# A graph-convolution kernel on one Trainium2 core: TensorE sums the last bucket ahead of the next bucket's counts, transposes and lookups

## The chip, the cores and the metric

The kernel runs on one core of one Trainium2 chip. A core has five engines with a queue of instructions each: TensorE (PE; its weight loads are listed apart as PEld), VectorE (DVE), ScalarE (ACT), GpSimd (POOL) and SyncE (SP). They run side by side and order themselves by semaphores. SBUF is the on-chip memory, PSUM (eight banks here, `bank[0]` to `bank[7]`) takes the results of matmuls, and DRAM is reached by DMAs. SP and POOL issue nearly all DMAs of this kernel. The metric is the device time of one launch in microseconds (us), lower is better.

## The reference, cut to what matters

There are 6250 nodes with 128 features, 200000 edges (src, dst, type), and 16 edge types.

```python
h = jnp.maximum(_layernorm(x, axis=-1), 0.0)
# inside the layer: src = edge source, rel = edge type, dst = edge target, embeddings = h
semb = embeddings[src] @ tokeys.T
oemb = embeddings[src] @ toqueries.T
pemb = relations[rel]
dots = jnp.sum(semb * pemb * oemb, axis=1) / e
values = jnp.exp(dots)
fr = src + n * rel
rowsum = jax.ops.segment_sum(values, fr, num_segments=r * n)
values = values / rowsum[fr]
msgs = values[:, None] * embeddings[dst]
output = jax.ops.segment_sum(msgs, fr, num_segments=r * n).reshape(r, n, e)
weights = jnp.einsum('rb,bij->rij', comps, bases_w)
out = jnp.einsum('rij,rnj->ni', weights, output)
x = x + jax.nn.relu(out)
```

Two edges with the same (src, type) have the same value, so the weight of an edge follows from how many edges of its type its source node has.

## The kernel before, in words

**Stage one** (up to about 420 us of the trace) sorts the edges by source into 49 buckets of 128 nodes (`NB = 49`), writes them to DRAM as records, and writes `Z`, the 16 transformed messages of each node, to DRAM.

**Stage two**, which the change touches, goes over the 49 buckets. A bucket has room for 36 tiles (`G = 36`) of 128 edges. In the order of one bucket b:

- SP (function `bucket`, lines 326 to 357) stores the rows of bucket b-2 when they are finished, joins two pieces of the record stream by a DRAM to DRAM DMA, waits for it, and loads the records of bucket b (`RL`).
- PE `turn_records` transposes them into PSUM (line 1277), DVE `records` and `gather_index` (lines 746, 784) make integers of them, the row numbers of Z among them.
- POOL `gather` (line 501) fetches one row of Z per edge, one indirect DMA for a tile. Tile 0 is shared with the bucket before and is not fetched. The page counts 1568 of these DMAs, 32 for a bucket. They fill one of two buffers, `Gbuf[par]`. A gather starts when PE has summed the bucket two before (`acc`), since that one used the same buffer.
- PE `tables` counts edges per node and type with one-hot matmuls (line 1286, 9 of them) and transposes the one-hot of types (line 1296, 18). DVE `own_counts` (792 to 798) takes its part of the counts. PE `sum_counts` (1307, 1308) finishes them.
- DVE `weights` (807 to 823) makes the weights. ACT `bucket` (line 1111) copies the transposes out of PSUM, spreads the one-hot of the next bucket (1088), and copies the shared tile between the gather buffers (`shared_tile`, 1101).
- PE `lookups` (line 1317, 18 matmuls in five groups) looks up each edge's weight, DVE `weighted_onehot` (line 833, 9 operations) puts it into the one-hot `OW`, and the two go in step: PE's group k waits for DVE's work on group k-2.
- PE `aggregate` (line 1329) sums weight times message over the 36 tiles into `bank[2]`. A float32 matmul shows as two passes, so this is 72 PE rows. DVE `finish` (line 841) adds x and applies the relu.

The loops are software pipelined. All orders are written by hand, one list for each engine, and each engine goes through its list in order. PE's list for one step b (`stepb`, lines 1343 to 1353) is: turn the records of b+1, tables of b, sum_counts of b, aggregate of b-1, lookups of b. DVE's list for a step b is: records and gather_index of b+1, own_counts of b, weights of b, tables of b+1 (one-hots, 753 to 776), finish of b-1, weighted_onehot of b. The change leaves DVE's list and SP's list as they are.

A gather's landing is told by semaphores. The tiles 1 to 29 (`PACED = 30`) raise one of four landing semaphores `land[q]`, by groups of eight tiles, and the tiles above raise `gat[par]`. POOL waits before each group of eight for the landing of the group two before it (lines 491 to 500). PE waits for each group before it sums it, and ACT waits for all before it copies the shared tile.

Of the kernel before, what the change touches and what calls it, by code (L numbers as in the profile page):

```python
# [32 lines left out]
def program(nc, x, src, dst, rel, tokeys, toqueries, relations, comps, bases_w, out):  # L33
# [16 lines left out]
    G = 36  # L50
# [23 lines left out]
    with ExitStack() as ctx:  # L74
# [308 lines left out]
        def _(pool):  # L383
# [96 lines left out]
            with pool.If(bad < 1):  # L480
                def gather(b, par, turn):
                    n = pool.value_load(ROWI[0:1, bass.ds(b, 1)], min_val=FLOOR, max_val=G)
# [7 lines left out]
                    def group_landed(b, q):  # L490
                        pool.wait_ge(land[q], (b + 1) * 16 * len(group_tiles[q]))
                        pool.sem_inc(s["pool_go"], 1)

                    def tile(k):
                        if k < PACED and k == group_tiles[k // GROUP][0]:

                            if k >= 2 * GROUP:
                                group_landed(b, k // GROUP - 2)
                            elif dyn(b) or b >= 1:
                                group_landed(b - 1, k // GROUP + 2)  # L500
                        g.indirect_dma_start(Gbuf[par][:, k, :], None, Z, bass.IndirectOffsetOnAxis(IDX[turn][:, k:k + 1], 0))\  # L501
                            .then_inc(land[k // GROUP] if k < PACED else gat[par], 16)
# [29 lines left out]
        def _(dve):  # L532
# [188 lines left out]
            chain(v.tensor_scalar(col(6), col(1), float(PACED), None, ALU.subtract), "nt")  # L721
# [235 lines left out]
        def _(act):  # L957
# [124 lines left out]
            with act.If(bad < 1):  # L1082
# [7 lines left out]
                def shared_tile(b, par):  # L1090
# [3 lines left out]
                    for q in range(4):  # L1094
                        act.wait_ge(land[q], (b + 1) * 16 * len(group_tiles[q]))
# [35 lines left out]
        def _(pe):  # L1131
# [121 lines left out]
            pe.wait_ge(s["nt"], 33)  # L1253
# [14 lines left out]
            with pe.If(bad < 1):  # L1268
# [53 lines left out]
                def aggregate(b, par):  # L1322
# [8 lines left out]
                    for q in range(4):  # L1331
                        pe.wait_ge(land[q], (b + 1) * 16 * len(group_tiles[q]))
                        for k in group_tiles[q]:
                            add(k, start=(k == FIRSTK))
# [4 lines left out]
                    add(0)  # L1339
                    for k in range(PACED, G):  # L1340
                        mm = add(k, stop=(k == G - 1))
                    mm.then_inc(s["acc"], 1)

                def stepb(b, par, rl_total):
                    if dyn(b) or b + 1 < NB:
                        turn_records(b + 1, 1 - par, rl_total)
                    if dyn(b) or b < NB:
                        tables(b, par)
                        sum_counts(b)
                    if dyn(b) or b >= 1:  # L1350
                        aggregate(b - 1, 1 - par)
                    if dyn(b) or b < NB:
                        lookups(b)
# [58 lines left out]
```

## Time and profile before

| | |
|---|---|
| median of 3 runs | 3075.16 us (3070.01 to 3075.73) |
| the profiled execution's own time | 3092.01 us |
| its span in the profile | 3090.2 us |
| mean granted TensorE clock | 0.674 of full speed |
| PE busy | 1511.4 us (49%) |
| PE weight loads busy | 1113.9 us (36%) |
| DVE busy | 1354.5 us (44%) |
| ACT busy | 462.4 us (15%) |
| POOL busy | 1652.3 us (53%) |
| mean DMA traffic | 55 GB/s, 170.48 MB |

The page gives each engine's busy time and its share of the span. No engine is busy for much over half of the span, so the time lies in waits. In a row of the page's fifth part, the two numbers behind the first bar are the busy time and the mean length of one instruction, and what stands behind the second bar is the idle time just before these instructions with what ended most of it. In a timeline each row has the start, the length, the engine, the line, and in square brackets the idle time before it and what ended it. "remote" says that the semaphore's update came at a time that fits no instruction's end, and "issue" that the profile shows nothing that was waited for. The end of a matmul is modelled, not recorded.

### The profile page before, as it was taken

The numbers are of one execution on the slowest core, as the hardware profiler recorded it, in microseconds if no ns is written. First come the engines' busy times: TensorE is split into PE (matmuls) and PEld (weight loads), VectorE is DVE, ScalarE is ACT, GpSimd is POOL, SyncE is SP. The second block draws the span as 40 slices with busy tenths as digits, with TensorE's granted clock in tenths as the row PEclk, the third lists the DMA queues.
The fourth block names the chain that finished last, engine by engine and source line by source line (L and its number), as shares of the span: only waits on it lengthen the run. The fifth ranks groups of instructions, "written<-read, shape, count | busy, mean of one in ns | idle before, by whom it ended". The sixth has DMA issues, their size and how long they took to land.

```text
span 3090.2 us, 33040 instructions
## 1 busy us (share of the span) xinstructions
PE 1511.4 (49%) x9072; PEld 1113.9 (36%) x9122; DVE 1354.5 (44%) x2384; ACT 462.4 (15%) x918; POOL 1652.3 (53%) x1804
## 2 busy tenths in 40 slices
PE   4999922444344444345444443444444444434345
PEld 3666612332233323233332332333332333323234
DVE  7999934334243433334243342434334343433333
ACT  4666601000010101000010100101000010100000
POOL 3444454655556464655646465564655556464653
PEclk8999965666666666656666666656656666666667
DMA  5444411111111111111111111111111111111111
GB/s 153 157 156 156 156 48 32 45 38 44 42 38 45 36 46 36 46 38 41 45 35 45 37 44 42 39 44 36 46 38 43 43 38 46 36 45 36 45 42 29
DMA packets 99826, 170.48 MB, mean 55 GB/s; under 512 B 32491, under 2 KB 48612, under 8 KB 99575
## 3 DMA queue, kind: packets, MB, share of 16 engines
q0 software_dynamic: 51776, 104.48, 13.1%
q1 hardware_dynamic: 47672, 65.57, 6.3%
q10 hardware_dynamic: 352, 0.14, 0.0%
q8 instruction: 10, 0.16, 0.0%
q14 instruction: 16, 0.13, 0.0%
HBM read 112.24 MB, written 59.59 MB: 56 GB/s over the span
## 4 chain that ended last, share of the span: by engine, by line
another core or an unknown queue 37%; issue 23%; DVE 19%; PE 15%; SPq 2%; DMA 1%; DVEq 1%; ACT 0%; POOLq 0%; ACTq 0%
PE bank L1209 6%; DVE arena L833 4%; DVE CX L798 3%; PE bank L1194 2%; DVE stage L776 2%; PE bank L1286 2%; DVE WC L809 1%; PE bank L1329 1%; DVE pay_all L792 1%; PE bank L1162 1%; DVE OHR L774 1%; PE bank L1317 1%; DVE pay_all L823 1%; DMA RL<-bucket_streams 1%
## 5 line engine op out<-in xcount | busy, mean ns | idle before, releaser
L501 POOL DMA_INDIRECT arena<-Z_messages,IDX x1568 | 1483.2, 946 | 1162.3 <-issue 967.3
L1329 PE MATMUL bank<-arena 128*128 128x128 f32 x3528 | 682.1, 350 | 696.4 <-issue 687.2
L1329 PEld LDWEIGHTS bank<-arena 128*128 128x128 f32 x3528 | 620.1, 260 | 759.3 <-issue 757.6
L807 DVE TENSOR_SCALAR WC<-bank 128x128 f32<-128x128 f32 x49 | 14.3, 292 | 1106.9 <-remote 1080.6
L1111 ACT COPY pay_all<-bank 128x1024 bf16<-128x1024 bf16 x147 | 108.0, 807 | 2152.5 <-remote 2131.8
L1317 PE MATMUL bank<-pay_all 128*128 128x256 bf16 x882 | 178.7, 346 | 309.0 <-DVE arena L833 236.6
L833 DVE TENSOR_TENSOR arena<-stage,bank 128x512 f32<-128x512 bf16 x441 | 268.8, 681 | 7.5 <-remote 7.1
L776 DVE TENSOR_TENSOR stage<-bank,NLF 128x4608 bf16<-128x4608 f32 x49 | 242.4, 4948 | 0.0
L1317 PEld LDWEIGHTS bank<-pay_all 128*128 128x128 bf16 x882 | 86.2, 113 | 383.6 <-DVE arena L833 292.1
L1286 PE MATMUL bank<-stage,OHR 128*128 128x512 bf16 (+1 forms) x392 | 176.3, 613 | 21.1 <-issue 16.7
L1209 PE MATMUL bank<-WT,HT 128*128 128x512 f32 x392 | 185.5, 613 | 0.0
L1277 PE MATMUL bank<-identf,RL 36*128 36x36 f32 x49 | 14.3, 291 | 338.9 <-DMA RL<-bucket_streams 228.2
L453 POOL DMA_INDIRECT bucket_streams<-REC,IDXW x50 | 54.2, 1084 | 199.4 <-ACT REC L1030 188.5
L792 DVE TENSOR_TENSOR pay_all<-bank,T 128x512 f32<-128x512 f32 x98 | 63.1, 686 | 203.7 <-issue 120.0
L1088 ACT COPY ORD<-OHR 128x2304 bf16<-128x2304 bf16 x49 | 103.5, 2112 | 268.8 <-DVE OHR L774 268.8
L746 DVE CAST RI<-bank 128x36 int32<-128x36 f32 x49 | 9.6, 196 | 299.3 <-PE bank L1277 166.6
L1277 PEld LDWEIGHTS bank<-identf,RL 36*128 36x128 f32 x49 | 8.8, 179 | 360.3 <-issue 360.3
L1042 ACT COPY stage<-bank 128x512 f32<-128x512 f32 x196 | 114.9, 586 | 35.7 <-PE bank L1209 34.6
L1307 PE MATMUL bank<-identf,VR 128*128 128x128 f32 x98 | 32.1, 423 | 160.0 <-DVE CX L798 95.6
L1286 PEld LDWEIGHTS bank<-stage,OHR 128*128 128x128 bf16 (+1 forms) x441 | 56.6, 138 | 127.9 <-issue 122.4
L1209 PEld LDWEIGHTS bank<-WT,HT 128*128 128x128 f32 x392 | 64.4, 189 | 82.5 <-ACT stage L1042 59.1
L798 DVE TENSOR_REDUCE CX<-pay_all 128x128 f32<-128x1024 f32 x49 | 91.4, 1865 | 0.0
(210 smaller groups left out, 1710.9 us busy)
## 6 DMA issues: line engine op xcount, KB each, us to landing
Z_messages<-stage SPq DMA_DIRECT2D x192, 256.0 KB
arena<-Z_messages,IDX POOLq DMA_INDIRECT x1568
X<-in_x SPq DMA_DIRECT2D x4, 768.0 KB, 12.9
out<-O SPq DMA_DIRECT2D x48, 64.0 KB
bucket_streams<-bucket_streams SPq DMA_DIRECT2D x97, 18.0 KB
arena<-in_L_gnn_bases_w SPq DMA_DIRECT2D x1, 1024.0 KB, 15.0
bucket_streams<-arena SPq DMA_DIRECT2D x1, 882.0 KB
RL<-bucket_streams SPq DMA_DIRECT2D x49, 18.0 KB
```

The costliest lines, as they stand in the source:

```text
L501: g.indirect_dma_start(Gbuf[par][:, k, :], None, Z, bass.IndirectOffsetOnAxis(IDX[turn][:, k:k + 1], 0))\
L776: v.tensor_tensor(OHN[par], over_b(iotaP, G), over_t(NLF[:], P), ALU.is_equal)\
L792: v.tensor_tensor(own8[:, 4 * h:4 * h + 4, :], bank[h][:, :].rearrange("p (t n) -> p t n", t=4), over_t(T8[:, 4 * h:4 * h + 4], P), ALU.mu ...
L798: v.tensor_reduce(CX[:], own8.rearrange("p t n -> p n t"), AX.X, ALU.add).then_inc(s["cx"], 1)
L833: v.tensor_tensor(OW[:, n:n + 4, :], OHN[par][:, n:n + 4, :], bank[LKB[k % 2][h]][:, :].rearrange("p (t n) -> p t n", t=4), ALU.mult)\
L1042: a.copy(ZS[par][:, k * 512:(k + 1) * 512], bank[4 + k % 2][:, :]).then_inc(s["z_sb"], 1)
L1088: a.copy(ORD[:], OHR[par][:].unsqueeze(2).broadcast_to([P, G, 4, R])).then_inc(s["ord"], 1)
L1111: a.copy(ORT[:, 8 * k:8 * k + n, :].rearrange("p k e -> p (k e)"), bank[TPB[k]][:, :].bitcast(BF16)[:, 0:n * P]).then_inc(s["oht"], 1)
L1209: t_.matmul(bank[4 + k % 2][:, :], HT[par][:], WT[:, 4 * k:4 * k + 4, :].rearrange("p r i -> p (r i)"), start=True, stop=True).then_inc(s[ ...
L1286: mm = t_.matmul(bank[k % 2][0:n * R, :], OHR[par][:, k // 2 * 8:k // 2 * 8 + n, :].rearrange("p k r -> p (k r)"), OHN[par][:, 4 * k:4 * k ...
L1317: mm = t_.matmul(bank[LKB[k % 2][m // 2]][:, m % 2 * 2 * P:(m % 2 + 1) * 2 * P], ORT[:, 4 * k + m, :], BD[:].rearrange("p t n -> p (t n)") ...
L1329: return t_.matmul(bank[2][:, 0:EMB], OW[:, k, :], Gbuf[par][:, k, :], start=start, stop=stop)
```

## The change

Four edits belong together.

- PE's list for a step is now: turn the records of b+1, aggregate b-1, tables of b, sum_counts of b, lookups of b. The aggregate comes first, ahead of the tables.
- In all buckets but the last, every tile raises `gat[par]`, the totals of `gat` in the number table are made for that (one more small DVE operation in the set-up, and the last bucket's total is less by the 29 paced tiles, counted with tile 0 as 30), and the landing groups remain only in the last bucket.
- PE waits once for the whole gather of the bucket, then for the shared tile, and sums the 36 tiles in one go, tile 0 first. Only in the last bucket does it still go group by group. ACT waits for `gat` alone.
- POOL no longer waits for the landing of earlier groups while it issues a gather.

```diff
             with pool.If(bad < 1):
                 def gather(b, par, turn):
+                    last = not dyn(b) and b == NB - 1
                     n = pool.value_load(ROWI[0:1, bass.ds(b, 1)], min_val=FLOOR, max_val=G)
                     pool.wait_ge(s["idx"], b + 1)
...
                     pool.sem_inc(s["pool_go"], 1)
 
-                    def group_landed(b, q):
-                        pool.wait_ge(land[q], (b + 1) * 16 * len(group_tiles[q]))
-                        pool.sem_inc(s["pool_go"], 1)
-
                     def tile(k):
-                        if k < PACED and k == group_tiles[k // GROUP][0]:
-
-                            if k >= 2 * GROUP:
-                                group_landed(b, k // GROUP - 2)
-                            elif dyn(b) or b >= 1:
-                                group_landed(b - 1, k // GROUP + 2)
                         g.indirect_dma_start(Gbuf[par][:, k, :], None, Z, bass.IndirectOffsetOnAxis(IDX[turn][:, k:k + 1], 0))\
-                            .then_inc(land[k // GROUP] if k < PACED else gat[par], 16)
+                            .then_inc(land[k // GROUP] if last and k < PACED else gat[par], 16)
...
-            chain(v.tensor_scalar(col(6), col(1), float(PACED), None, ALU.subtract), "nt")
+            chain(v.tensor_scalar(col(6), PARI[:, 0:1], float(NB - 1), float(1 - PACED), ALU.is_equal, ALU.mult), "nt")
+            chain(v.scalar_tensor_tensor(out=col(6), in0=col(1), scalar=-1.0, in1=col(6), op0=ALU.add, op1=ALU.add), "nt")
...
                     g_total = act.value_load(ROWI[0:1, bass.ds(b + (1 + par) * NB, 1)], min_val=16 * (FLOOR - PACED), max_val=16 * G * (NB + 1) // 2)
-                    for q in range(4):
-                        act.wait_ge(land[q], (b + 1) * 16 * len(group_tiles[q]))
                     act.wait_ge(gat[par], g_total)
...
-            pe.wait_ge(s["nt"], 33)
+            pe.wait_ge(s["nt"], 34)
...
-                    for q in range(4):
-                        pe.wait_ge(land[q], (b + 1) * 16 * len(group_tiles[q]))
-                        for k in group_tiles[q]:
-                            add(k, start=(k == FIRSTK))
+                    if not dyn(b) and b == NB - 1:
+                        for q in range(4):
+                            pe.wait_ge(land[q], 16 * len(group_tiles[q]))
+                            for k in group_tiles[q]:
+                                add(k, start=(k == FIRSTK))
+                        rest = range(PACED, G)
+                    else:
+                        rest = range(FIRSTK, G)
                     pe.wait_ge(gat[par], g_total)
                     pe.sem_inc(s["pe_go"], 1)
                     if dyn(b) or b >= 1:
                         pe.wait_ge(s["shared"], b)
-                    add(0)
-                    for k in range(PACED, G):
+                    add(0, start=(rest[0] == FIRSTK))
+                    for k in rest:
                         mm = add(k, stop=(k == G - 1))
                     mm.then_inc(s["acc"], 1)
 
                 def stepb(b, par, rl_total):
                     if dyn(b) or b + 1 < NB:
                         turn_records(b + 1, 1 - par, rl_total)
+                    if dyn(b) or b >= 1:
+                        aggregate(b - 1, 1 - par)
                     if dyn(b) or b < NB:
                         tables(b, par)
                         sum_counts(b)
-                    if dyn(b) or b >= 1:
-                        aggregate(b - 1, 1 - par)
-                    if dyn(b) or b < NB:
                         lookups(b)
```

What stands on TensorE in the loop over buckets, before. `identf,RL` is turn_records, `stage,OHR` and `identb,ORD` are tables, `CX,RS` is sum_counts, `arena` is aggregate, `pay_all` is lookups.

```order
L1277 MATMUL bank<-identf,RL 128x36 [waits s_w]
L1286 MATMUL bank<-stage,OHR 128x512 [waits s_ow]
L1296 MATMUL bank<-identb,ORD 128x128 [waits s_ord,s_oht]
L1308 MATMUL bank<-CX,RS 128x128
L1329 MATMUL bank<-arena 128x128 [waits s_land0]
L1329 MATMUL bank<-arena 128x128 [waits s_land1]
L1329 MATMUL bank<-arena 128x128 [waits s_land2]
L1329 MATMUL bank<-arena 128x128 [waits s_land3]
L1329 MATMUL bank<-arena 128x128 [waits s_gat1,s_shared]
L1317 MATMUL bank<-pay_all 128x256 [waits s_bd]
```

The same place of TensorE's list in the changed kernel (its lines are 10 lower):

```order
L1267 MATMUL bank<-identf,RL 128x36 [waits s_w]
L1319 MATMUL bank<-arena 128x128 [waits s_gat1,s_ow,s_o,s_shared]
L1319 MATMUL bank<-arena 128x128 x35
L1276 MATMUL bank<-stage,OHR 128x512 [waits s_ow]
L1286 MATMUL bank<-identb,ORD 128x128 [waits s_ord,s_oht]
L1298 MATMUL bank<-CX,RS 128x128
L1307 MATMUL bank<-pay_all 128x256 [waits s_bd]
```

The 36 tiles of the sum moved from behind the counts to ahead of them, right behind the turn of the next records, and four waits inside the sum went.

What GpSimd issues for one bucket in the loop, before:

```order
L501 DMA arena<-Z_messages,IDX 128x128 [waits s_land2]
L501 DMA arena<-Z_messages,IDX 128x128 x6
L501 DMA arena<-Z_messages,IDX 128x128 [waits s_land3]
L501 DMA arena<-Z_messages,IDX 128x128 x7
L501 DMA arena<-Z_messages,IDX 128x128 [waits s_land0]
L501 DMA arena<-Z_messages,IDX 128x128 [waits s_land1]
```

And in the changed kernel, for the same bucket:

```order
L492 DMA arena<-Z_messages,IDX 128x128 [waits s_acc,s_shared]
L492 DMA arena<-Z_messages,IDX 128x128 x29
L496 COMPARE_AND_BRANCH
L492 DMA arena<-Z_messages,IDX 128x128
```

The waits for landings went, and nothing else of it moved.

## Rows read from the trace of the kernel before

**Rows 1.** The page's costliest groups: DVE's first weight operation, ACT's copies of transposes.

```profile
L807 DVE TENSOR_SCALAR WC<-bank 128x128 f32<-128x128 f32 x49 | 14.3, 292 | 1106.9 <-remote 1080.6
L1111 ACT COPY pay_all<-bank 128x1024 bf16<-128x1024 bf16 x147 | 108.0, 807 | 2152.5 <-remote 2131.8
```

**Rows 2.** Timeline of PE, one bucket: start, length, line, count, idle before.

```profile
1516.36 0.29 PE L1277 MATMUL bank<-identf,RL 36*128 36x36 f32 x1 [4.56 <-DMA RL<-bucket_streams]
1517.01 3.76 PE L1286 MATMUL bank<-stage,OHR 128*128 128x512 bf16 x8 [0.36 <-issue]
1520.70 1.56 PE L1296 MATMUL bank<-identb,ORD 128*128 128x128 bf16 x18
...
1524.90 0.58 PE L1308 MATMUL bank<-CX,RS 128*128 128x128 f32 x2
1525.71 2.96 PE L1329 MATMUL bank<-arena 128*128 128x128 f32 x13 [0.23 <-issue]
...
1535.58 0.37 PE L1329 MATMUL bank<-arena 128*128 128x128 f32 x1 [2.43 <-issue]
...
1549.59 6.88 PE L1329 MATMUL bank<-arena 128*128 128x128 f32 x49 [0.33 <-issue]
```

**Rows 3.** Timeline of DVE, the same bucket.

```profile
1507.24 0.28 DVE L841 SCALAR_TENSOR_TENSOR O<-bank,X 128x128 f32<-128x128 f32 x1
...
1522.38 1.86 DVE L798 TENSOR_REDUCE CX<-pay_all 128x128 f32<-128x1024 f32 x1
1549.70 0.29 DVE L807 TENSOR_SCALAR WC<-bank 128x128 f32<-128x128 f32 x1 [25.45 <-remote]
...
1553.65 0.73 DVE L823 SCALAR_TENSOR_TENSOR pay_all<-W,X,WC 64x128 bf16<-64x128 bf16 x2
...
1561.43 0.28 DVE L841 SCALAR_TENSOR_TENSOR O<-bank,X 128x128 f32<-128x128 f32 x1
1561.63 5.48 DVE L833 TENSOR_TENSOR arena<-stage,bank 128x512 f32<-128x512 bf16 x9
```

**Rows 4.** Timeline of ACT, the same bucket.

```profile
1549.72 2.20 ACT L1111 COPY pay_all<-bank 128x1024 bf16<-128x1024 bf16 x3 [44.91 <-remote]
```

**Rows 5.** Timeline of POOL: one gather's first and last tile, the next one's first.

```profile
1504.61 0.95 POOL L501 DMA_INDIRECT arena<-Z_messages,IDX  x1 [14.63 <-issue]
...
1543.38 0.95 POOL L501 DMA_INDIRECT arena<-Z_messages,IDX  x1 [0.30 <-issue]
1557.37 0.95 POOL L501 DMA_INDIRECT arena<-Z_messages,IDX  x1 [13.05 <-issue]
```

**Rows 6.** Chain of waits, 1400 to 1620 us: SP's table reads (start, length).

```profile
1508.43 0.28 SPq L321
...
1512.03 0.70 SPq L326
```

**Rows 7.** Timeline of SP, next bucket: store of finished rows, load of records.

```profile
1561.91 0.39 SPq L357 DMA_DIRECT2D out<-O  x1
...
1583.69 0.71 SPq L327 DMA_DIRECT2D RL<-bucket_streams  x1
```

**Rows 8.** Timeline of PE, next bucket, whose records came late.

```profile
1582.02 0.29 PE L1277 MATMUL bank<-identf,RL 36*128 36x36 f32 x1 [16.03 <-DMA RL<-bucket_streams]
...
1604.34 9.23 PE L1329 MATMUL bank<-arena 128*128 128x128 f32 x56 [1.02 <-issue]
```

**Rows 9.** Timeline of PE: first bucket's sum, end of the last but one's, last's.

```profile
525.83 9.36 PE L1329 MATMUL bank<-arena 128*128 128x128 f32 x72
...
3062.69 7.04 PE L1329 MATMUL bank<-arena 128*128 128x128 f32 x40 [1.72 <-issue]
...
3075.80 10.97 PE L1329 MATMUL bank<-arena 128*128 128x128 f32 x72 [1.40 <-DVE arena L833]
```

**Rows 10.** Stretches: length, PE, PEld, DVE, ACT, POOL busy (instructions), clock, DMA share, GB/s.

```profile
560.00:565.00 5.00, 0.64 (x2) 0.31 (x2) 0.00 (x0) 0.00 (x0) 3.78 (x5) 0.74 0.20 52
...
580.00:585.00 5.00, 4.63 (x18) 3.91 (x18) 2.95 (x9) 2.20 (x3) 0.00 (x0) 0.50 0.00 0
```

## The prediction, made before the changed kernel ran

> **What bounds the kernel now.** I read the page first, for who waits. DVE's first weight operation was idle 1106.9 us ahead of its 49 instructions, and ACT's copies of the transposes 2152.5 us, and both waits are put down to "remote" [rows 1]. What DVE waits for there is sum_counts, and ACT the transposes, both of them PE's. So I read one bucket engine by engine. PE ended the transposes at 1522.26 (1520.70 plus 1.56) and sum_counts at 1525.48 [rows 2]. DVE went on at 1549.70 [rows 3] and ACT at 1549.72 [rows 4], within 0.02 us of each other and 24 to 27 us after PE had finished. In between PE itself nearly stood still: 13 passes of the sum went in 2.96 us, then ten passes with up to 2.4 us of idle before each, and from 1549.59 the last 49 in 6.88 us [rows 2]. Three engines are let go in the same 0.15 us. That is no wait of the program, it is PE's completions coming through late.
>
> Next I asked what else has these borders. POOL's gather runs from 1504.61 to 1544.33 [rows 5]. The flow returns 45.0 us after the gather's first DMA and 5.3 us after its last. SP shows the other border: a read of the number table takes 0.28 us at 1508.43 and 0.70 us at 1512.03 [rows 6], 7.4 us into the gather. Between the two stores and loads of SP, from 1561.91 to 1583.69, the same few steps [rows 7] that are quick early in a gather take 20 us. While a gather runs the DMA engines are busy only 0.20 of the time, and once it is over they are idle while PE bursts [rows 10], so transfer bandwidth isn't it. I call the time from 7 us into a gather until 45 us into it the thin stretch: PE's and SP's steps pass at 0.7 us each [rows 6] to 1.4 (a load and a matmul in the 0.37 plus 2.43 us [rows 2]), after a first few dozen rows of PE's that still pass. DVE shows none of it: 5.48 us for nine operations [rows 3] holds in both.
>
> The period follows. From the end of one sum, 1503.7 (0.9 before rows 5's first DMA), to the end of the next, 1556.47, it is 0.9 to start the gather, 45.0 to the end of its thin stretch, 6.9 for the remaining passes. Over 47 periods, from 535.19 to 3069.73 [rows 9], the mean is 53.9 us. The gather's own 40 us, the sum of all engines' work and the landing waits end nothing.
>
> **What the change takes away, adds and moves.** I count from the end of a sum (0), the next gather starts at 0.9 and flow returns at 46.0.
>
> *The landing waits on POOL, ACT and PE.* POOL's DMAs stand 1.25 us apart (1543.38 less 1504.61, over 31), waits or not, and the sum of b-1 reads a gather that ended a whole period earlier. Price 0. Bounds: if unpaced gathers emptied the thin stretch altogether the bound would be rival 2, if they widened it, the 7.4 us before it begins could go, which costs where sum_counts is caught in it (rival 3). One small DVE operation in the set-up is 0.3 us at most by DVE's rows.
>
> *The sum ahead of the tables.* This turns the order of a period round. Before, weights were ready long before they were asked for, and between two sums stood lookups, DVE's one-hots, the next records, the tables. Now between sum b-1 and sum b stand, in this order: tables of b, 3.76 plus 1.6 us [rows 2]; DVE's own counts, 1520.77 to 1524.24, 3.5 us [rows 2, 3], overlapping the transposes; sum_counts, 1.3 us, out at 8.5. That is about where the thin stretch begins (8.3 from the end of the sum), and PE's first few dozen rows in it pass, so ACT and DVE should get these two signals in time. That is the change's gain: the waits of rows 1 all but go. Then DVE: weights 4.7 us (1549.70 to 1554.38), its one-hots for the next bucket 7.0 us (to 1561.43), only then finish of b-1, at 20.5, and from 20.8 the weighted one-hots with PE's lookups, 5.5 us at best [rows 3], so 26.3.
>
> But these last ones fall into the thin stretch. Three lookup groups of 4, 4 and 2 matmuls with their loads, some 25 rows with PE's register steps, stand behind waits for DVE, and DVE waits for each of them. At 0.7 us they cost 10 to 17 us: 36 to 43.
>
> *SP, which the diff doesn't touch, is moved most.* It loads the records of b+2 behind the store of b-1, which waits for DVE's finish of b-1. Before, finish came 3.5 us after the sum (1507.24 against 1503.7), 2.7 into the gather, and the records' turn at 1516.36, 9.1 later. Now finish comes at 20.8, well inside the thin stretch. Started 4.5 us into the gather, the same steps brought the records to PE at 1582.02 [rows 8], 20.1 after the store [rows 7]. SP issues some 25 instructions there, two DMAs and their landings among them. Started at 21, all of them are thin: from 17.5 us (25 by 0.7) over 20 (rows 7 and 8's own, which began before the stretch did) to 35 (25 by 1.4), less what the flow's return at 46.0 spares. The records arrive between 38 and 48, and I take 46.5: the row's 20 had a quick start, and PE's lookups now want the same stretch. Price of this step in the old order was 0, hidden under the sum; in the new order PE turns b+2's records directly ahead of sum b, so whoever is last gives the sum's start: 47.0.
>
> *The sum itself* then runs whole. 72 passes took 9.36 and 10.97 us outside gathers [rows 9], and bursts after an idle stretch 0.14 to 0.165 us a pass (49 in 6.88, 56 in 9.23) [rows 2, 8], 10.1 to 11.9 for 72. The granted clock of the stretch after such a wait is 0.50 [rows 10], the 1.2 GHz level, so I take 11.5. Before, 23 of the 72 had gone through before the flow came back, and that head start is what is lost.
>
> Period: 47.0 + 11.5 = 58.5 against 53.9.
>
> *Ends.* The first sum can start at 517.6, behind the first lookups, instead of 525.8, and ends 6.6 us earlier, 528.6. In the last period no records are turned, the lookups' 36 to 43 gives the start, so it is some 53. After the sum of bucket 47 the last bucket's whole chain now follows: before, 20.5 us (3090.2 less 3069.73), now 13 more for tables, counts and weights, 33.5.
>
> Sum: 528.6 + 46 x 58.5 + 53 + 33.5 = 3306 of span, plus 1.8 around it, 3308 by the profile's own time. The profiled execution (3092.0) was 0.55% above the median 3075.16, so the median comes to 3290.
>
> On PE's run-ahead the Trainium skill, "TensorE: Matmul & The Clock Gate", section "Architectural detail: the array is 16× 32×32, not 1× 128×128", gives TensorE's queue as 64 instructions deep. That agrees with the trace as I read it: behind the held transposes stood 8 rows of sum_counts and about 46 of the sum. By that rule 32 passes with their loads would fit, were the queue empty when sum b starts inside the thin stretch, 9 more than rows 2's 23, and rival 1's sum would gain 1.3 us a period on them.
>
> The same skill, "Trainium Kernel Development and Optimization", section "Key Constraints", says that DMAs of SP, ACT and POOL run on the same 16 engines and interleave. It speaks against dropping the pacing: SP's small loads would stand among more gathers. At the share of 0.20 [rows 10] it adds nothing I can price, and the sum leaves it out.
>
> **The rivals.**
>
> 1. *The sum gets its head start, slightly faster.* Place: SP's loads in the thin stretch. If they pass at 0.7 us a step or less, the records are there by 38, the lookups as well, and PE puts 30 passes through or into its queue before 46.0. Then 42 remain, 7.0 us, and the period is 53.0: 528.6 + 47 x 53.0 + 33.5 = 3053, a median of 3038. It decides at a start of the sum before about 41; at 44 the period is 56 and the time 3175. For it: rows 7 and 8's stretch took 20 us, part of it thin. Against it: that stretch began at 4.5, where the first steps pass quickly.
> 2. *The thin stretch goes with the pacing.* Then POOL's 32 x 1.25 + 0.9 = 41 us is the period: 528.6 + 47 x 41 + 33.5 = 2489, 2477 by the median. Against it: nothing in the rows ties the 7.4 us or the 45.0 us to a landing wait.
> 3. *sum_counts is caught in the thin stretch.* It needs to come out by about 8.5 and the stretch opens at 8.3 or a little before. If it is held to 46.0, weights, one-hots and weighted one-hots (17.2 us) and the sum follow: 75 a period, 4045. Held by half, with its 22 rows at 0.7 us, DVE ends 15 us later, SP's finish too, and the sum starts at 53: 64.5, 3565. For it: the transposes and sum_counts are more rows than the few dozen. Against it: rows 2's counts, issued 12.4 us into a gather, were still picked up at once, since DVE's own counts were done 3.5 us behind them [rows 3].
>
> **Chances.** Forecast with its middle (3140 to 3400): 0.62. Rival 1 (below 3140): 0.20, two thirds of it faster. Rival 2: 0.04. Rival 3: 0.14. The range for 8 in 10 is 3050 to 3520, and the forecast's own is 3140 to 3400. A difference under 0.2% can't be told from none in this kernel. Faster by more than that 0.17, within it 0.03, slower by more 0.80.
>
> **What would show it.** In the profile after: ACT's copies of transposes start within a few us of the transposes (the 2131.8 of "remote" gone), DVE's first weight operation likewise, 3 to 4 us behind the counts. DVE's finish stands 20 us behind the sum's last pass, not 3.5. PE's turn of the records waits for the records' DMA and stands 44 to 48 us behind the sum, with the sum in one row of x72, 10 to 12 us long. POOL's gaps between gathers grow from 13 to 18 us. SP's steps from the store to the load take 20 us or more. The forecast is wrong if the turn of the records isn't late, if the sum shows 20 to 30 passes ahead of the flow's return, or if SP's steps inside a gather take 0.3 us.

## The result, and the profile after

The changed kernel took 3284.4 us (median of 4, 3281.8 to 3287.03), the kernel before 3075.09 (median of 4) beside it: a ratio of 1.069, 95% interval 1.0677 to 1.0702. Forecast were 3290 us and slower. The profiled execution has a span of 3283.8 us, where the steps of the prediction gave 3306, and a mean granted clock of 0.657.

The sum over the periods, by the trace after: first sum done at 528.0 (forecast 528.6), 46 periods of 58.17 (58.5), a last one of 48.8 (53), and 31.2 behind it (33.5). Before, the mean period was 54.0.

The page's costliest groups after, to be held against [rows 1] (its lines are 8 to 10 lower):

```profile
L492 POOL DMA_INDIRECT arena<-Z_messages,IDX x1568 | 1485.4, 947 | 1343.6 <-PE bank L1319 858.0
L1319 PE MATMUL bank<-arena 128*128 128x128 f32 x3528 | 515.7, 319 | 62.5 <-issue 44.1
L1267 PE MATMUL bank<-identf,RL 36*128 36x36 f32 x49 | 14.2, 290 | 1094.3 <-DMA RL<-bucket_streams 1094.3
L1101 ACT COPY pay_all<-bank 128x1024 bf16<-128x1024 bf16 x147 | 108.0, 807 | 2225.2 <-PE bank L1286 2174.0
```

DVE's first weight operation no longer appears among the large waits: of its 1106.9 us of idle all but some 50 have gone (45.8 us over 42 buckets, shown with E10). In their place PE itself waits 1094.3 us ahead of 49 turns of records, for the records' DMA. ACT still idles as long as before, but now because the transposes come late in the period, not because their signal does. A total of idle time doesn't tell these two apart, the timeline does.

One bucket after, PE, DVE, ACT and SP (start, length, line, count, idle before), beside [rows 2 to 4, 7]:

```profile
1505.11 10.29 PE L1319 MATMUL bank<-arena 128*128 128x128 f32 x72 [0.87 <-issue]
1515.23 2.22 PE L1276 MATMUL bank<-stage,OHR 128*128 128x512 bf16 x9
1517.39 1.18 PE L1286 MATMUL bank<-identb,ORD 128*128 128x128 bf16 x18
...
1519.05 2.20 ACT L1101 COPY pay_all<-bank 128x1024 bf16<-128x1024 bf16 x3 [45.47 <-PE bank L1286]
...
1521.69 0.39 PE L1298 MATMUL bank<-CX,RS 128*128 128x128 f32 x2
1522.11 0.29 DVE L799 TENSOR_SCALAR WC<-bank 128x128 f32<-128x128 f32 x1 [1.07 <-PE bank L1298]
...
1534.00 0.28 DVE L833 SCALAR_TENSOR_TENSOR O<-bank,X 128x128 f32<-128x128 f32 x1
1534.19 3.69 DVE L825 TENSOR_TENSOR arena<-stage,bank 128x512 f32<-128x512 bf16 x6
1534.48 0.40 SPq L357 DMA_DIRECT2D out<-O  x1
...
1545.06 1.29 DVE L825 TENSOR_TENSOR arena<-stage,bank 128x512 f32<-128x512 bf16 x2 [7.18 <-remote]
1550.66 0.69 DVE L825 TENSOR_TENSOR arena<-stage,bank 128x512 f32<-128x512 bf16 x1 [4.31 <-remote]
1552.88 0.70 SPq L322 DMA_DIRECT2D bucket_streams<-bucket_streams  x1
1561.32 0.38 SPq L327 DMA_DIRECT2D RL<-bucket_streams  x1
1563.18 0.29 PE L1267 MATMUL bank<-identf,RL 36*128 36x36 f32 x1 [24.63 <-DMA RL<-bucket_streams]
```

From the sum's last pass at 1515.40: the weights begin at +6.7 with their signal prompt, finish at +18.6, the weighted one-hots are done at +36.0, the turn comes at +47.8 and the next sum starts at 1564.31. POOL's gaps between gathers:

```profile
1516.20 0.95 POOL L492 DMA_INDIRECT arena<-Z_messages,IDX  x1 [18.03 <-PE bank L1319]
...
1574.83 0.95 POOL L492 DMA_INDIRECT arena<-Z_messages,IDX  x1 [18.91 <-PE bank L1319]
```

And the chain of waits there (start, length, what), inside the gather that began at 1516.20: each step of SP's, idle or not, is 0.70 us or twice that, where early in a gather the same table read took 0.28 [rows 6]:

```profile
1539.41 0.70 SPq L333
1540.11 0.70 issue
...
1560.58 0.70 SPq L326
1561.32 1.62 DMA RL<-bucket_streams
1562.98 0.04 issue
1563.03 0.05 SPq L321
```

The last step of 0.70 us ends at 1561.28, 45.1 us behind the gather's first DMA, and from the next step after the records' landing, at 1562.98, they are 0.04 us. The stretches of that bucket (length, PE, PEld, DVE, ACT, POOL busy, clock, DMA share, GB/s): while the stretch lasts, PE is busy for 4.56 of 38 us at the 1.2 GHz level, and the DMA engines at 0.19.

```profile
1523.00:1561.00 38.00, 4.56 (x18) 2.01 (x18) 15.86 (x28) 2.31 (x2) 25.00 (x27) 0.50 0.19 50
1564.00:1574.00 10.00, 9.69 (x73) 9.68 (x74) 0.08 (x1) 0.00 (x0) 0.00 (x0) 0.83 0.01 2
```

### The profile page after: what moved, and what is told of

The parts are those of the page before. It is cut to its first block, busy times and chain, and to the rows that moved or that the text cites. A ratio compares the mean times of both kernels' runs of the same rounds, so it can differ in the third digit from the quotient of the medians.

```text
span 3283.8 us, 32426 instructions
## 1 busy us (share of the span) xinstructions
PE 1307.7 (40%) x9121; PEld 984.4 (30%) x9122; DVE 1367.4 (42%) x2385; ACT 462.9 (14%) x918; POOL 1654.5 (50%) x1804
## 4 chain that ended last, share of the span: by engine, by line
issue 57%; SPq 22%; PE 14%; DVE 4%; DMA 2%; another core or an unknown queue 1%; DVEq 0%; ACT 0%; POOLq 0%; ACTq 0%
SPq L322 6%; PE bank L1199 5%; SPq L321 5%; SPq L326 3%; PE bank L1319 3%; PE bank L1184 2%; SPq L362 2%; SPq L333 1%; DMA RL<-bucket_streams 1%; PE bank L1152 1%; SPq L327 1%; DVE stage L768 1%; SPq L337 1%; SPq L341 1%
## 5 line engine op out<-in xcount | busy, mean ns | idle before, releaser
L1319 PE MATMUL bank<-arena 128*128 128x128 f32 x3528 | 515.7, 319 | 62.5 <-issue 44.1
L1319 PEld LDWEIGHTS bank<-arena 128*128 128x128 f32 x3528 | 506.9, 234 | 69.6 <-issue 67.9
L825 DVE TENSOR_TENSOR arena<-stage,bank 128x512 f32<-128x512 bf16 x441 | 277.3, 683 | 526.2 <-remote 416.5
L1307 PE MATMUL bank<-pay_all 128*128 128x256 bf16 x882 | 223.6, 414 | 632.8 <-DVE arena L825 321.5
L1267 PE MATMUL bank<-identf,RL 36*128 36x36 f32 x49 | 14.2, 290 | 1094.3 <-DMA RL<-bucket_streams 1094.3
L1307 PEld LDWEIGHTS bank<-pay_all 128*128 128x128 bf16 x882 | 99.2, 132 | 743.6 <-DVE arena L825 370.9
L1276 PE MATMUL bank<-stage,OHR 128*128 128x512 bf16 (+1 forms) x441 | 110.9, 387 | 0.0
L1184 PE MATMUL bank<-pay_all,stage 125*80 125x100 f16 x1600 | 81.5, 208 | 2.3 <-DVE stage L655 2.3
L1184 PEld LDWEIGHTS bank<-pay_all,stage 125*80 125x80 f16 x1600 | 78.8, 117 | 2.4 <-DVE stage L655 2.4
L1297 PE MATMUL bank<-identf,VR 128*128 128x128 f32 x98 | 24.3, 333 | 133.3 <-DVE CX L790 103.4
```

The costliest lines, as they stand in the source:

```text
L825: v.tensor_tensor(OW[:, n:n + 4, :], OHN[par][:, n:n + 4, :], bank[LKB[k % 2][h]][:, :].rearrange("p (t n) -> p t n", t=4), ALU.mult)\
L1184: mm = t_.matmul(DM[:, h * NS:(h + 1) * NS], OHS[par][:, t, :], PAY[par][:, t, :, :].rearrange("p x b -> p (x b)"), start=(t % HC == 0), s ...
L1276: mm = t_.matmul(bank[k % 2][0:n * R, :], OHR[par][:, k // 2 * 8:k // 2 * 8 + n, :].rearrange("p k r -> p (k r)"), OHN[par][:, 4 * k:4 * k ...
L1307: mm = t_.matmul(bank[LKB[k % 2][m // 2]][:, m % 2 * 2 * P:(m % 2 + 1) * 2 * P], ORT[:, 4 * k + m, :], BD[:].rearrange("p t n -> p (t n)") ...
L1319: return t_.matmul(bank[2][:, 0:EMB], OW[:, k, :], Gbuf[par][:, k, :], start=start, stop=stop)
```

## The experiments

They ran in five sessions, and the sessions fall into two kinds. In the second and third the kernel before took 3085.6 and 3072.0 us. In the first, fourth and fifth it took 2393.0, 2392.9 and 2396.9, the same program, each time with spreads of 6 us or less. I call them the thin and the free sessions; the first result (3075.09) is of the thin kind. The second (thin) and the fifth (free) list the same chip number, so what decides between them isn't known.

### Thin sessions

**E7, the changed kernel again.** No edit.

> The changed kernel itself, in one session with the kernel before. The first four experiments ran where the kernel before took 2393 us and not 3075, and where PE's and SP's steps weren't slowed while a gather ran; GpSimd's 32 DMAs of 1.25 us a bucket were then the bound. Theory A (the loss is nothing but SP's record load caught in the thin stretch): where the kernel before takes about 2393, finish of b-1 stands 20.5 us behind the sum, the records' turn 9.1 us later, the sum takes 0.9 and 10, together 40.5 us, just GpSimd's own 40.2 to 41, so 2390 to 2430, a ratio of 1.00 to 1.015. Where the kernel before takes about 3075, 3284 again. Rival B (the new order costs by itself, through a longer chain of PE and DVE work): the 4 us a bucket stay in any session, so 2393 + 49 x 4 = 2590.

Measured: 3300.15 us against 3085.6, ratio 1.0699 (1.0681 to 1.0717). The first result again; the question of the free session stayed open, since this one was thin.

**E11, PE's order alone.** The kernel before, with

```diff
+                    if dyn(b) or b >= 1:
+                        aggregate(b - 1, 1 - par)
                     if dyn(b) or b < NB:
                         tables(b, par)
                         sum_counts(b)
-                    if dyn(b) or b >= 1:
-                        aggregate(b - 1, 1 - par)
```

> The kernel before with only PE's order changed (sum of b-1 ahead of tables of b); landing groups and all waits stay. Theory A (the order is the whole loss): where the kernel before takes 3075 to 3086, 1.065 to 1.075 of it, 3280 to 3310. Theory C (the whole sums and the lost pacing carry part of it, a quarter or more): 1.02 to 1.05. If the kernel before takes 2393, 2393 again.

Measured: 3286.77 against 3072.03, ratio 1.0697 (1.0679 to 1.0715). Theory A: the order is all of it. Its page has the wait of the changed kernel:

```profile
L1277 PE MATMUL bank<-identf,RL 36*128 36x36 f32 x49 | 14.2, 290 | 1098.8 <-DMA RL<-bucket_streams 1088.1
```

Landing groups, POOL's pacing and whole sums move nothing that can be measured, as their price of 0 said. (The reverse, old order with whole sums, ran only in a free session, E2.)

**E10, finish first.** The changed kernel, with SP's store and load let go early:

```diff
+                    if dyn(b) or 1 <= b:
+                        finish(b - 1, 1 - par)
                     own_counts(b)
...
-                    if dyn(b) or 1 <= b:
-                        finish(b - 1, 1 - par)
```

> The changed kernel with DVE's finish of b-1 put ahead of its own counts of b, on a chip where (if it is as in the last session) the kernel before takes 3075 to 3086 and the changed one 1.070 of it. Theory A (the loss comes from SP's record load, that starts 21 us behind the sum because it waits for finish): finish comes about 1 us behind the sum, SP's steps start early in the gather and end before 20 us, the turn of the records no longer sets the start of the sum; the lookups with DVE's weighted one-hots do (36 by the trace of the changed kernel, a little later for the 0.3 us of finish), or flow's return where they are held. Sum to sum 36 to 46 plus 0.9 plus 10, so 47 to 56: 528 + 47 x 51.5 + 31 = 2980, range 2790 to 3150, clearly under the changed kernel's 3300. Theory B (the sum's place inside the stretch is what costs, whoever starts it): no change, 3270 to 3310. If the kernel before takes 2393, 2393 again and nothing is told.

Measured: 3250.82, ratio 1.0585 (1.0567 to 1.0602). Both theories missed. A wanted 2790 to 3150, B no change, and some 35 us came (36 against E11 of the same session, which has the changed kernel's ratio). The mechanism that A named was indeed removed; something else ended only 0.7 us ahead of it. Timeline of E10: a gather's first DMA, weights, lookups and weighted one-hots beside it, then the sum and SP's store and load for the next bucket:

```profile
1498.09 0.94 POOL L492 DMA_INDIRECT arena<-Z_messages,IDX  x1 [17.52 <-PE bank L1319]
...
1508.89 0.29 DVE L799 TENSOR_SCALAR WC<-bank 128x128 f32<-128x128 f32 x1 [6.07 <-remote]
...
1513.61 1.89 PE L1307 MATMUL bank<-pay_all 128*128 128x256 bf16 x8 [9.76 <-DVE pay_all L815]
...
1520.87 1.27 DVE L825 TENSOR_TENSOR arena<-stage,bank 128x512 f32<-128x512 bf16 x2
...
1530.02 1.28 DVE L825 TENSOR_TENSOR arena<-stage,bank 128x512 f32<-128x512 bf16 x2 [7.87 <-remote]
...
1540.52 1.28 DVE L825 TENSOR_TENSOR arena<-stage,bank 128x512 f32<-128x512 bf16 x2 [9.22 <-remote]
1541.86 0.61 PE L1307 MATMUL bank<-pay_all 128*128 128x256 bf16 x2 [9.46 <-DVE arena L825]
...
1545.41 10.19 PE L1319 MATMUL bank<-arena 128*128 128x128 f32 x72 [2.69 <-DVE arena L825]
...
1556.34 0.39 SPq L357 DMA_DIRECT2D out<-O  x1
...
1562.02 0.68 SPq L327 DMA_DIRECT2D RL<-bucket_streams  x1
```

SP now goes from the store to the load in 5.7 us instead of 26.8 after. But the counts' signal reached DVE's weights late (6.07 us of "remote" here), and each round of the weighted one-hots, PE to DVE and back, took 9.2 to 10.5 us (1520.87 to 1530.02 to 1540.52). Over 43 periods the first lookups stand 13.5 us behind the sum in E10 and 11.5 in the changed kernel, and the last weighted one-hot ends at 47.0 and at 35.3. The waits for PE and DVE in E10:

```profile
DVE arena L825 <- remote: 829.9, 124, 9.9
...
PE bank L1307 <- DVE arena L825: 703.3, 93, 10.2
...
DVE WC L799 <- remote: 103.2, 21, 7.4
```

In the changed kernel DVE's rows are

```profile
DVE arena L825 <- remote: 397.3, 70, 7.4
...
DVE WC L799 <- PE bank L1298: 45.8, 42, 1.6
```

So in E10 the stretch held the counts' signal as well: DVE waited more than 1.7 us for it in 28 of 46 buckets, at most 7.4, and in none of the changed kernel's. All that moved ahead of that signal are SP's steps and DVE's finish (0.29 us); why this brings PE's signals under the stretch earlier isn't shown.

Over 43 periods the next sum started 47.9 us behind the last in the changed kernel and 47.2 in E10, though the turn came at 39.2 on average instead of 46.8.

**E12, weighted one-hots before the next one-hots.** E10, with DVE's `weighted_onehot(b)` moved ahead of `tables(b + 1)`, 7 us earlier.

> The kernel of e10 with DVE's weighted one-hots of b put ahead of its one-hots of b+1, 7 us earlier, at 13 us behind the sum instead of 20. Theory A: more of the lookups pass early in the gather, lookups are done at 27 to 36, sum to sum 38 to 50, 2600 to 2950 us and 50 to 150 us below e10. Theory B (any order of DVE's is the same, since the lookups wait for flow's return): equal to e10 within 0.5 per cent. If the kernel before takes 2393, 2393 again.

Measured: 3249.79, ratio 1.0585, equal to E10. Sum starts at 47.2 again. This refutes A's second half and bears out B's result. B's reason, that the lookups wait for the flow's return, is off: PE's last lookup stood at 38.6 us on average, and it was the signals to DVE that came late, its last weighted one-hot ending at 47.1. Three times now (changed kernel, E10, E12) another chain or another order of it stood ahead of the sum, and each time it ended when the stretch did.

**E9, 18 gathers a bucket instead of 32.** The kernel before, with

```diff
                     def tile(k):
+                        if 2 * GROUP <= k < PACED:
+                            return
```

and the landings of those groups no longer waited for.

> The kernel before with tiles 16 to 29 not gathered (their messages are left out; the sum runs over what lies in the buffer): about 18 indirect DMAs a bucket instead of 32. Theory A: GpSimd needs 18 x 1.25 = 22.5 us a bucket, so in a session at 2393 the bound moves to the chain of DVE and PE (DVE is busy 27.6 us a bucket, 1354.5 over 49), 29 to 33 us a bucket, 1880 to 2050 us. In a session at 3075 the thin stretch lasts until 5.3 us behind the last DMA, so the period is 0.9 + 22.5 + 5.3 + 6.9 = 35.6, some 2210 us. Rival: the stretch isn't set by the number of DMAs, then 3075 stays within 3 per cent.

Measured: 2211.18, ratio 0.717 (0.7146 to 0.7194), on the 2210 that was worked out from 0.9 + 22.5 + 5.3 + 6.9; the mean period is 35.9 against 35.6. Its terms fit less well. In the median bucket the flow returns 25.6 us after the gather's first DMA, not 27.8, and the rest of the sum takes 8.2 us, not 6.9, since only 14 passes are through instead of 23: 34.7 in all. Seven of the 46 buckets took 41.5 to 45.7 us, as their sum started 31 to 35 us behind the last with no pass through, and they bring the mean up. That the total agrees to 0.3 us is in part luck. Timeline of its POOL, one gather's first and last DMA and the next's first, and DVE and ACT at the stretch's end:

```profile
1491.65 0.95 POOL L500 DMA_INDIRECT arena<-Z_messages,IDX  x1 [13.11 <-issue]
...
1512.92 0.94 POOL L500 DMA_INDIRECT arena<-Z_messages,IDX  x1 [0.30 <-issue]
1526.29 0.95 POOL L500 DMA_INDIRECT arena<-Z_messages,IDX  x1 [12.43 <-issue]
```

```profile
1517.22 0.29 DVE L806 TENSOR_SCALAR WC<-bank 128x128 f32<-128x128 f32 x1 [6.48 <-remote]
1517.24 2.20 ACT L1110 COPY pay_all<-bank 128x1024 bf16<-128x1024 bf16 x3 [25.73 <-remote]
```

DVE and ACT get PE's signals within 0.02 us of each other here too, 3.4 us behind the end of the last DMA of 18, where it was 5.3 behind the last of 32 [rows 3 to 5]. So the stretch's end moved with the gather's last DMA: with 14 DMAs fewer (17.5 us) the flow came back 25.6 us after the first DMA instead of 45.1. In a thin session it is the gather that times the stretch.

### Free sessions

**E1 to E4**: E1 is the edit of E10, E2 the changed kernel with PE's old order (whole sums, no landing groups), E3 the edit of E11, E4 that of E12.

> The changed kernel with one move on VectorE: finish of b-1 (the operation that SyncE's store and load wait for) stands ahead of own_counts of b, not behind the one-hots for b+1. Theory A (SyncE's load of the records, started 20 us late and inside the thin stretch, sets the start of the sum): the records are turned about 10 us behind the sum instead of 47.8, the sum then starts when the lookups are done, about 36 us behind the sum before, gets some 30 of its 72 passes through before the flow returns at 46, and the period falls from 58.0 to 53 to 54: 3030 to 3060 us. Theory B (TensorE itself can't get the sum through while a gather runs, whatever the records do): the sum still ends 10 us behind the flow's return, 58 a period, 3280 us.

> The changed kernel with TensorE's order put back (tables, sum_counts, then the sum of b-1, then lookups); whole sums, no landing waits on GpSimd, landing groups only in the last bucket stay. If the loss lies in the order alone, this is the kernel before within 0.5%: 3060 to 3090 us. If dropping the pacing and the groups costs by itself (SyncE's small DMAs among more gathers, an earlier or thinner stretch), it lies above 3100.

> The kernel before with only TensorE's order changed (sum of b-1 ahead of tables of b); the landing groups and GpSimd's pacing stay. If the order is the whole of the change: 3270 to 3300 us, as the changed kernel. If the groups still help a sum that starts late, they could save at most the 0.9 us before the sum: 3240.

> As e1_finish_first, and VectorE also makes the weighted one-hots of b straight behind the weights of b, with the one-hots for b+1 behind them. Theory A: the lookups start 7 us earlier and without SyncE's steps beside them, the sum starts 20 to 27 us behind the sum before, some 45 passes are through when the flow returns, 25 remain (4 us): a period of 50 to 51, 2880 to 2930 us. Theory B: no change against e1.

Measured: 2392.15, 2393.34, 2392.9 and 2392.46 against 2393.01, ratios 0.9997, 1.0, 1.0 and 0.9998, each with an interval of about 0.001 either way. Every expectation's time was written for a kernel of 3075 and missed; that E2 equals the kernel before and E4 equals E1 came true, but here all of them are equal. What they show is what the order costs without the stretch. E3's timeline, one store, load, turn and sum:

```profile
1201.35 5.48 DVE L833 TENSOR_TENSOR arena<-stage,bank 128x512 f32<-128x512 bf16 x9
1201.64 0.39 SPq L357 DMA_DIRECT2D out<-O  x1
...
1206.68 0.38 SPq L327 DMA_DIRECT2D RL<-bucket_streams  x1
1208.88 0.29 PE L1277 MATMUL bank<-identf,RL 36*128 36x36 f32 x1 [3.17 <-DMA RL<-bucket_streams]
...
1209.98 8.83 PE L1329 MATMUL bank<-arena 128*128 128x128 f32 x58 [0.82 <-issue]
1220.94 3.07 PE L1329 MATMUL bank<-arena 128*128 128x128 f32 x14 [2.13 <-DMA arena<-Z_messages,IDX]
```

Store to turn takes 7.2 us, nine weighted one-hots 5.48, all in the middle of a gather. The sum catches up with the gather and waits 2.13 us for its last tiles: GpSimd is the bound, 32 x 1.25 = 40 us a bucket. The chain on E3's page has it in front, and gives the landing:

```profile
POOL 46%; issue 24%; PE 15%; DMA 12%; POOLq 1%; DVE 1%; SPq 0%; ACT 0%; ACTq 0%; DVEq 0%
```

```profile
arena<-Z_messages,IDX POOLq DMA_INDIRECT x1568, 2.5
```

That is rival 2's period and nearly its time (2477), in the kernel before as in the others, but by the session and not by the change. The Trainium skill, "Perfetto Trace Analysis", section "DMA Instruction — SWDGE (GPSIMD)", says that such an instruction's shown end is that of writing its descriptors, not of the transfer. The trace agrees: 0.94 us an instruction, 2.5 to landing. The changed kernel unaltered ran in no free session. E1 differs from it only in where finish stands.

**E13, E14, E15, the gather let go early.** The kernel before; PE signals behind tile 29 (E13, E15) or 23 (E14), POOL starts on that signal and waits for the whole sum only ahead of the next tile:

```diff
-                        pool.wait_ge(s["acc"], b - 1)
+                        pool.wait_ge(s["part"], b - 1)
...
+                        if k == EARLY and (dyn(b) or b >= 2):
+                            pool.wait_ge(s["acc"], b - 1)
...
+                            if k == EARLY - 1:
+                                mm.then_inc(s["part"], 1)
```

> The kernel before, with GpSimd's gather of b let go when PE has summed tiles 1 to 29 of b-2 instead of all 36 (the whole sum is waited for ahead of tile 30). 14 of 72 passes are left then, 14 x 0.14 = 2.0 us. Theory A (the period is 0.9, 45 us from the gather's first DMA to the flow's return, and the rest of the sum; nothing between two gathers' borders counts): each period is 2.0 us shorter, 3075 - 47 x 2.0 = 2981, ratio 0.965 to 0.975 where the kernel before takes 3070 to 3086. Theory B (what stands between sum and tables is as tight: weighted one-hots, SP's load and the tables get caught in the stretch, which opens 7 us into the gather): the head start of 23 passes goes or the tables' 60 rows pass at 0.7 us, 3100 to 3300. Where the kernel before takes 2393 (GpSimd bound), no change.

> The same with the gather let go behind tile 23: 26 passes are left, 3.7 us. Theory A: 3075 - 47 x 3.7 = 2901, ratio 0.94 to 0.95. Theory B, as in the experiment beside it, more so: 3150 to 3400. If A holds for 2 us and B for 4, the slack between the sum's end and the stretch's start lies between them. Where the kernel before takes 2393, no change.

> The kernel of e13 once more, in the hope of a chip on which the kernel before takes 3070 to 3086. Theory A (only the gather's borders and the rest of the sum count): 2.0 us off each of 47 periods, ratio 0.965 to 0.975, 2970 to 3010. Theory B (the steps between the sum and sum_counts have no slack of 2 us before the stretch opens): 1.00 to 1.07. Where the kernel before takes 2393, 2393, and the question stays open.

Measured: 2393.34 and 2393.4 against 2392.93, and 2396.77 against 2396.92. All in free sessions, so no change, as each expectation says for that case, and inconclusive for what they were made for. Whether they shorten the 3075 is open. E8, a gather by half rows (half the bytes, as many DMAs), gave no result, since the indexed row of such a DMA has to be contiguous. So bytes against number of DMAs is open too: E9 cut both.

## Why the prediction was right, and where it wasn't

- *The total*: nearer than its parts. The sum of the steps, 3306 of span, was 22 us too long. The 0.55% that was then taken off, because the profiled execution before had been above its median, wasn't there after (3285.58 profiled, 3284.4 the median). So 3290 lies within 6 us by luck, and the steps themselves within 0.7%.
- *The bound, the thin stretch*: right for the sessions it was made in. Period = 0.9 + stretch + rest of the sum holds with each term measured (over 43 buckets before, 0.9 + 45.4 + 7.7 = 54.0), and E9 shows the middle term following the gather.
- *The waits of weights and transposes go*: right for the weights (+6.7, forecast by 8.5). ACT's signal was prompt (0.5 us behind the transposes by the rows above), but its idle total stayed.
- *Landing waits, price 0*: right, E11 against E7, 1.0697 and 1.0699. Rival 2 is refuted with it: without the pacing the stretch stayed, and where it was absent (E3) the pacing was there.
- *Rival 3* (sum_counts caught): not in the changed kernel, where the longest wait was 1.6 us, but in 28 of E10's 46 buckets, in part.
- *SP's load caught in the stretch, turn at 46.5*: measured at 46.8 on average over 43 periods (45.0 to 48.6). From store to load SP took 26.8 us, between the 17.5 and 35 given. The load goes out within a microsecond of the flow's return, so this row alone doesn't tell whether the count of steps or the border sets it. E10 does: with SP's steps out of the way, the sum starts 0.7 us earlier.
- *The rows that SP's step was sized by* were read too trustingly. In rows 7 and 8 the load of the records is shown at 1583.69, behind the turn of these very records at 1582.02. That is so in 12 of 49 buckets before, while in E2 and E3 the turn always stands at least 1.7 us behind its load. So the times shown in the stretch, SP's or PE's, are not quite when things happened, by some 3 us here.
- *The sum, 11.5*: mis-sized. It measured 10.4 (mean of 43) at a mean granted clock of 0.79, not the 0.50 I chose it by. In the bucket above the clock stood at 0.50 until 1567, 3 us into the sum, and at 1.00 from 1569 on. The other way went 0.9 us between turn and sum (0.87 of "issue"), which wasn't priced. Together the period came out at 58.17 for 58.5.
- *The last period, 53*: mis-sized, 48.8. The sum could start at 34.0, not at some 41, I left out that a sum which starts there has its head start again, and the last bucket's gather has 30 DMAs, so that the flow returned 42.1 us after its first DMA. PE's rows of it, from the timeline after, 35 passes ahead of the flow's return and 36 behind it:

```profile
3237.70 7.11 PE L1319 MATMUL bank<-arena 128*128 128x128 f32 x35 [10.98 <-DVE arena L825]
3245.94 0.27 PE L1319 MATMUL bank<-arena 128*128 128x128 f32 x1 [1.13 <-issue]
3246.65 5.91 PE L1319 MATMUL bank<-arena 128*128 128x128 f32 x36 [0.44 <-issue]
```

  That is rival 1's mechanism, with more than its 30 passes, in the one period of this kernel where nothing else stood ahead of the sum. The prediction's 54 rows behind the held transposes (23 passes) measure no queue: here 35 passes with their loads, 70 rows, went in one go, and in the kernel before 15 to 24 passes were through in the loop's buckets, the fewer the later the sum started. The end was 31.2 for 33.5.
- *"The new order's loss is SP's, the lookups follow at 36 to 43"*: the forecast nearly held (35.3 on average), but the ranking of causes was weak. It reads as though an early finish would win back what is over 43. E10 gave 0.7 us of start and some 35 us in all, since with SP's steps out of the way the lookups and weighted one-hots started 2 us later and took until the stretch's end. The cause that the runs bear out is one level up: before, the stretch fell on a sum that was already queued, with some 21 passes through and nothing to be answered; now the sum stands behind work that needs answers between engines, which isn't done until the stretch is over. The loss of 4.2 us a period is, over 43 buckets of each trace, 2.7 us of head start (10.4 of sum instead of the 7.7 that were left at the flow's return; 6.9 in rows 2's bucket) and 1.5 us ahead of the sum, which starts 47.9 behind the last one where the flow had returned at 46.3: what the turn and the sum's start take.
- *Rival 1* (records there by 38) can be read off E10: the turn came at 29 to 47, and still 40 of 46 sums had no head start. It had left the rounds of the lookups, 9 to 10 us each, out. E10's second sum, where the signals weren't late, started at 36.4, some 37 passes were through when the flow came back, and the period was 51.8: the rival's mechanism and nearly its 53.

What stays open is what the stretch is. It holds PE's and SP's steps and PE's signals, not DVE's work, ACT's or POOL's, begins about 7 us into a gather (by 5.8 in E10's bucket above, where the counts ended at 1503.86 and their signal was held) and ends 3 to 6 us behind its last DMA, and three sessions of five had none. The Trainium skill, "NOTIFIC — the notification-queue block", section "7.1 Overflow: three behaviours, one of which stalls the engine", says that the internal pipeline for engines' records always holds its producers back rather than lose one. By that rule slow taking of records could hold engines back; it gives no time for it, and doesn't say why SP and PE and not DVE. The shown times that are out of order, and the landing records that are missing (below), say that the recording is disturbed in the stretch, not that it causes it. No run here shows that it is this, nor what the kernel takes unrecorded.

## What to carry to other kernels

Where a long stretch of slow issue can't be avoided, put into it the one block of work that is already queued and needs no answer from another engine, and keep out of it everything that goes to and fro: here that was worth 7%. Removing the wait that a profile names gains only up to the next chain that ends at the same border; ask what the border itself is before pricing the wait. And run the kernel before beside every experiment: here its own time changed by 22% between sessions, and the change's ratio with it.

## What the runs showed of the hardware that was not expected

- One program, 3072 to 3086 us in two sessions of experiments (3075 in the first result's) and 2393 to 2397 in three, stable within each; two of them, one of either kind, list one chip number.
- In the thin kind SP's single steps take 0.70 us or twice that, 0.02 to 0.5 in the free kind (E3, from store to turn); a round between PE and DVE takes 9.2 to 10.5 us (E10) instead of the 1.2 between two groups of lookups in E3. The change of pace comes from one step to the next.
- In the thin kind a profile can show an effect ahead of its cause: the records' turn on PE starts ahead of SP's load of them in 12 of 49 buckets before, by up to 1.7 us, where in E3 it never stands less than 1.7 us behind it.
- In the thin kind most records of the gathers' landings are missing from the trace (the first landing semaphore has 2305 updates of 5488 before, all 5488 in E3's free session), and the page gives no landing time, where in the free kind it gives 2.5 us. A missing landing time on a page was thus a sign of the kind.
